# mLSTM heads of a four-layer forward pass: two extra 128x512 matmuls on TensorE for each head, into an idle PSUM bank

## The reference

```python
logfg = jax.nn.log_sigmoid(f_pre)
Fcum = jnp.cumsum(logfg, axis=-1)
Dmat = Fcum[..., :, None] - Fcum[..., None, :] + i_pre[..., None, :]
Dmat = jnp.where(causal, Dmat, -jnp.inf)
m = jnp.max(Dmat, axis=-1, keepdims=True)
Smat = jnp.exp(Dmat - m)
qk = jnp.einsum('bhsd,bhtd->bhst', q, k) / jnp.sqrt(jnp.float32(dqk))
C = qk * Smat
n = jnp.maximum(jnp.abs(jnp.sum(C, axis=-1, keepdims=True)), jnp.exp(-m))
h = jnp.einsum('bhst,bhtd->bhsd', C / n, v)
```

## Time and profile before

| | |
|---|---|
| runs, median (lowest to highest) | 750.74 us (750.07 to 752.1) |
| the profiled execution's own time | 753.29 us |
| its span, first to last instruction | 751.5 us |
| mean granted TensorE clock, share of full speed | 0.935 |
| PE busy | 712.5 us, 95% of the span |
| DVE, ACT, POOL busy | 443.5, 423.5, 252.0 us |
| stage of the 32 heads | 517.04 to 619.98 us, 102.94 us |

### The profile page before, as it was taken

How to read it: one execution, slowest core, us unless ns; L and a number is a source line. 1 busy time by engine, 2 the same in 40 slices (tenths; PEclk the granted TensorE clock), 3 DMA queues, 4 the chain that set the end, 5 groups by cost and what they waited for, 6 DMA issues and landing times. The chain is left out here.

```text
span 751.5 us, 15356 instructions
## 1 busy us (share of the span) xinstructions
PE 712.5 (95%) x5290; PEld 670.3 (89%) x5290; DVE 443.5 (59%) x961; ACT 423.5 (56%) x1106; POOL 252.0 (34%) x265
## 2 busy tenths in 40 slices
PE   8999999999999999999987999988998799999995
PEld 8999999999999999999877999987666579999995
DVE  6465665576655766566565655643155437655686
ACT  5566686667756677666684333366454544333553
POOL 3624742244422434224741411217254122111011
PEclk9999999999999999999999999998556659999998
DMA  6266644456343663436500400007320100000000
GB/s 228 72 209 196 174 131 123 119 167 176 118 119 100 181 181 102 131 96 185 169 3 4 159 2 0 15 11 235 113 69 15 44 0 1 2 0 0 1 28 28
DMA packets 44889, 69.63 MB, mean 93 GB/s; under 512 B 3376, under 2 KB 30640, under 8 KB 44592
## 3 DMA queue, kind: packets, MB, share of 16 engines
q1 hardware_dynamic: 44416, 68.31, 30.4%
q10 hardware_dynamic: 432, 0.79, 0.3%
HBM read 52.18 MB, written 16.91 MB: 92 GB/s over the span
## 5 line engine op out<-in xcount | busy, mean ns | idle before, releaser
L303 PE MATMUL PJ<-xTh,WBh 128*128 128x256 f32 x364 | 106.6, 293 | 0.4 <-POOL WBl L808 0.4
L305 PE MATMUL PJ<-xTh,WBl 128*128 128x256 f32 x364 | 102.7, 282 | 0.0
L304 PE MATMUL PJ<-xTl,WBh 128*128 128x256 f32 x364 | 102.7, 282 | 0.0
L545 ACT ACTIVATE probs<-SC,nmax 128x256 f32<-128x256 f32 x128 | 59.5, 471 | 63.9 <-DVE nmax L671 62.4
L793 POOL TENSOR_TENSOR stage<-stage 128x256 f32<-128x256 f32 x32 | 24.5, 765 | 164.1 <-DVE stage L659 164.1
L669 DVE TENSOR_REDUCE rmax<-SC 128x2 f32<-128x512 f32 x64 | 44.2, 691 | 54.4 <-PE SC L384 47.5
L1154 PE MATMUL UG<-xTh,WBh 128*128 (+1 forms) x256 | 73.5, 287 | 1.1 <-PEq L49 1.1
L552 ACT ACTIVATE probs<-probs,rinv 128x256 f32<-128x256 f32 x128 | 58.5, 509 | 27.2 <-DVE rinv L675 27.1
L1157 PE MATMUL UG<-xTh,WBl 128*128 (+1 forms) x256 | 72.4, 283 | 0.0
L1155 PE MATMUL UG<-xTl,WBh 128*128 (+1 forms) x256 | 72.4, 283 | 0.0
L303 PEld LDWEIGHTS PJ<-xTh,WBh 128*128 128x128 f32 x364 | 69.2, 190 | 1.0 <-issue 0.6
(11 more groups left out here) (252 smaller groups left out, 2453.4 us busy)
## 6 DMA issues: line engine op xcount, KB each, us to landing
K<-scr_k SPq DMA_DIRECT2D x60, 256.0 KB, 4.5
raw<-in_w_att SPq DMA_DIRECT2D x37, 256.0 KB, 4.7
Q<-scr_q SPq DMA_DIRECT2D x15, 512.0 KB, 7.4
stage<-scr_m SPq DMA_DIRECT2D x4, 1024.0 KB, 5.9
scr_q<-rot_h SPq DMA_DIRECT2D x30, 128.0 KB
scr_q<-rot_l SPq DMA_DIRECT2D x30, 128.0 KB
scr_k<-rot_h SPq DMA_DIRECT2D x30, 128.0 KB
scr_k<-rot_l SPq DMA_DIRECT2D x30, 128.0 KB
```

What stands on the lines that cost most here:

```text
L303: pe.matmul(out, ah, bh, start=(i == 0), stop=False)
L304: pe.matmul(out, ah, bl, start=False, stop=False)
L305: last = pe.matmul(out, al, bh, start=False, stop=(i == n - 1))
L545: last = act.activation(probs[:, j % 2, t, :], SC[j % 2][:, t, :], ACT.Exp, scale=SCALE, bias=nmax[:, j % 2, t:t + 1], accum_out=rsum[:, j ...
```

## The change

A function `busy(c, h)` is added to PE's stream. It is called in `heads` between `scores(c, h + 1)` and `values(c, h)`. It multiplies columns 0 to 127 of `WLh[:, 0]` with the 512 columns of `WLh[:, 1]`, twice, and writes bank `TB`. Nothing reads that result.

For chunks 2 and 3 it is left out at head 5, where ACT and DVE read `TB`, and at heads 6 and 7 it first waits for `xt_split`, that is until DVE has read `TB`. So there are 30 calls and 60 added matmuls. No other engine's stream changes.

```diff
@@ layers @@
         MLP_PIECES = (3, 2, 2)
+        BUSY = 2
...
+            def busy(c, h):
+                if c >= 2 and h == AT["T"] + 1:
+                    return
+                if c >= 2 and h > AT["T"]:
+                    pe.wait_ge(s_["xt_split"], N_T[2] + c - 1)
+                for _ in range(BUSY):
+                    pe.matmul(TB[:, :], WLh[:, 0, 0:P], WLh[:, 1, :], start=True, stop=True)
+
             def back(c, pair):
...
                 for h in range(HM):
                     if h + 1 < HM:
                         scores(c, h + 1)
+                    busy(c, h)
                     values(c, h)
                     if h == 0 and c:
                         back(c - 1, 3)
```

## The result

The changed kernel took 758.3 us, the median of 10 runs (753.3 to 765.4), against 751.2 us before (ten runs again, where the 750.74 us above was of three). The ratio is 1.0088, with a 95% interval from 1.0063 to 1.0112; it leaves out the two slowest of the ten, which lie over 1.5% above the fastest. The time lies inside my range of 732 to 760, but on the other side of no change from the forecast of 740.

What follows compares the result with a forecast made beforehand. PE at the low clock was taken to bound the heads' stage. Chunk gains of 3 + 3 + 1 + 4 = 11 us from 750.7 gave 740 us; eight-in-ten range 732 to 760, the forecast's own 735 to 745.

Steps and rivals of the forecast that it cites:

- What bounds the stage, and the drop of the clock in the first wait: Heads' stage: PE sets the pace, at 1.2 GHz after a 2.93 us wait; a head costs 2.46 us, 1.45 at 2.4 GHz.
- So I take it that the pair raises the clock within a head or two wherever PE has work: All heads: the added whole-array pair lifts PE to 2.4 GHz, though long waits still drop it; such a head gains 0.65 us.
- The price of a pair: Each added pair on PE's path costs 0.46 us at the high clock and 0.92 us at the low one.
- rival B: The pair does not raise the clock; 21 exposed pairs cost 0.92 us each, 770 us; chance 0.18.
- Chunk 0: First chunk of heads: PE-bound 18.8 us becomes 14.3, less 1.5 for a slow head; gain 3.0 us.
- Chunk 1: Second chunk: gain 2 before `norm_b` and 3 after it, less 2 for a clock fall; gain 3.0 us.
- Chunk 2: Third chunk: nothing shorter up to 584.31; the 9.5 us behind gain 3, less 2 for the clock; gain 1.0 us.
- Chunk 3: Last chunk: 2.4 us from earlier values plus 3 in the tail, less 1.4 for low clock; gain 4.0 us.
- C, a clock that swings: Heads: the pair raises the clock but idle time drops it every few heads; about 750 us; chance 0.14.
- A, the clock that never falls: Heads: the clock never falls back inside them, so 18 us are gained, 733 us; chance 0.13.
- The rule of the Trainium skill: Heads' low stretch: busy time alone would give 2.4 GHz at over 93% records; the trace shows 1.2 GHz.

Runs made afterwards that it cites:

- second profile: The changed kernel profiled once more with no edit; this profiled run took 756.93 us.
- first profile: The changed kernel's first profiled execution, the slowest of its ten runs, 765.35 us.
- the twelve products on 32 rows: Kernel before the change, plus 12 products on 32 of 128 array rows in chunk 0's first wait, none elsewhere: 750.6 us, ratio 0.9945.

## Why the prediction was wrong, point by point

- **What bounds the stage, and the drop of the clock in the first wait: right.** The run with that wait filled and nothing else gained 8 us and turned chunk 0 from 22.4 into 14.4 us. A head at the high clock was put at 1.45 us and measured 1.37. In chunks 1 and 2 PE sets the pace only in part: with the waits filled they ran at 2.4 GHz throughout, and with pairs still took 23.9 and 26.1 us, against 27.0 and 27.4 before.
- **"So I take it that the pair raises the clock within a head or two wherever PE has work": this step failed.** It took 23.9 us of low clock, seven heads, in both profiles, and three products a head still needed 17 us. I had read the rise in the projection as a matter of the kind of product, the whole array against 32 rows or 33 columns. The columns were the wrong thing to look at, as the pair on 33 columns shows; and one rise during twelve products in a row says nothing about two products in a head. What exactly the rise takes stays open.
- **What I never asked: whether the heads hold the high clock by themselves.** The rows had heads at the high clock in chunk 2, but with waits of 1.4 us before both values, and I took the fall at 572.26 for a property of the heads. Without the waits they hold it. With this the pair is not needed on the path: the kernel with filled waits takes 741.8, 738.5 and 734.3 us with two, one and no product a head.
- **The price of a pair was undersized.** I took 0.46 and 0.92 us from the step of products in a stream. Measured are 0.66 and 1.15 us. The difference, 0.2 us at either level, is the passage from the last 512-column product to the next values, which a stream does not show. At the low clock one, two and three products put the values off by 0.73, 1.15 and 1.58 us: 0.43 each and 0.30 once. So a head with a pair gains about 2.72 - (1.37 + 0.16 + 0.66) = 0.53 us at the high clock and loses 1.15 at the low one, and some two in three of the exposed heads would have had to run high to come out even (1.15/1.68, an estimate). Even by my own 0.65 and 0.92 it was six in ten, not the half that stands under rival B.
- **Chunk 0: 3.0 us gained in the forecast, 6.8 lost.** Seven pairs at 1.15 us, less the short high stretches at its ends. This term alone turns the sum.
- **Chunk 1: 3.0 gained in the forecast; 0.6 gained and 0.8 lost in the two profiles.** The clock was high up to `norm_b` and fell in its wait, as I said. But behind it, it stayed low for 6.8 and 10.2 us, most of the tail, with the larger price on each pair there; I had taken back 2 of 3 us.
- **Chunk 2: 1.0 gained in the forecast; 2.4 and 1.7 lost.** `norm_b` began 12.2 us after the chunk's first scores, before and after, as expected: nothing up to there depends on the clock. What I missed lies behind. The gating at the end of `norm_b` took 1.63 us instead of 0.69, with POOL's weight split (1.45 us from 590.75) beside it now, as in chunk 1 before, and then the tail ran low, with two pairs at the full price. DVE's timeline in the second profile:

```profile
586.02 5.06 DVE L1749 TENSOR_TENSOR ho<-hraw,hsc 128x256 f32<-128x256 f32 x2 [1.79 <-POOL hsc L1855]
591.11 1.63 DVE L1754 TENSOR_TENSOR ho<-ho,x 128x512 f32<-128x512 f32 x1
```

- **Chunk 3: 4.0 gained in the forecast; 5.4 gained in one profile, 4.5 lost in the other.** I had taken back 1.4 us for a stretch of low clock; without it the step gives 5.4, which is what the profile without a fall measured.
- **The rivals.** C, a clock that swings, at 750 us, came nearest, and its reason was right in part: waits drop it, behind `norm_b` in chunks 1 and 2 and in the first profile at the start of chunk 3. But it fell at most once a chunk, not every few heads, and each time stayed low for 6.8 to 23.9 us. B, that the pair does not raise it, is what chunk 0 did. A, the clock that never falls, was reached only with the waits filled, and then at 741.8 us with the pairs, 734.3 without.
- **The rule of the Trainium skill.** "TensorE: Matmul & The Clock Gate", section "What's actually happening", puts the clock down to how busy the engine was. I set it aside since the heads' records fill the low stretch. For the fall it was the better guide: all falls within the heads but one come in a wait of PE or at most 1.8 us behind it. The exception is the fall at 521.35 behind the twelve products on 32 rows, which PE's records fill. The same page, in the table of "Why this matters for your kernels", says to leave no long idle gaps between bursts of matmuls, and that is the kernel that won; but between heads waits of 1.4 us were long enough here, and in chunk 3 of the first profile 0.70 and 0.78 us. The length of the wait alone does not decide: the second profile held through the same two, and the kernels with filled waits held through 1.85 us (one product a head, chunk 1) and 1.71 us (none, chunk 2). For the rise the section does not tell which work counts.

## What to carry to other kernels

Where a stage runs at the low clock, look first for the wait behind which it fell, and fill that wait with products into an idle bank; there they cost nothing as long as they end before the wait does, while the same products among the real ones cost their time and the passage to the next. Ask whether the real stream holds the high level by itself before paying to hold it: one run with only the first wait filled answers that. And a stream that cannot raise the clock may well keep it, so that one short wait can cost a whole stage.

## What the runs showed of the hardware that I had not expected

- The level depends on the past. The same heads of chunk 0 ran at 1.2 GHz from 521.05 to 539.45 before the change, and at 2.4 GHz to the chunk's end behind a filled wait, with PE's records without a gap in both.
- What goes before a rise: with a pair on 33 of 128 columns it came at the same head as with a pair on all (chunk 1 at 0.87 in both), in plain float32 too. With a pair on 32 of 128 rows it did not come in chunks 0 and 1 (0.50) and did in chunks 2 and 3.
- Products on different groups of 32 rows run at the same time: the pair on 32 rows starts 0.02 us behind scores on another group, and the head costs 2.58 us instead of 3.6.
- A program that stands near the edge has two times: 743 and 751 us with the twelve products on 32 rows, 20.7 and 30.7 us in the last chunk of the changed kernel behind the same two waits.
